# A transformer block on one core: butterfly weights laid out by partition, first steps reordered, second row group in the last score slots

## What is computed

```python
x = x + 0.5 * ffn(layernorm(x))
x = x + attention(layernorm(x))      # 16 heads of 16, causal, 4096 rows
x = x + 0.5 * ffn(layernorm(x))      # the same weights again
def ffn(x):
    h = butterfly(x @ W_exp + b_exp, up_weights)      # 1024 wide, 10 stages
    h = gelu(h + up_bias)
    return butterfly(h, down_weights) @ W_con + b_con + down_bias
def butterfly(y, weights):           # stage s pairs feature i with i + 2**s
    for stage in range(10):
        a, b = the two members of each pair; w = the pair's 2x2 matrix
        y = (w00 * a + w01 * b, w10 * a + w11 * b)
```

## Time and profile before

| what | value |
|---|---|
| median of 3 runs | 2031.27 us (2030.27 to 2039.89) |
| the profiled execution: its time | 2032.39 us |
| its span in the profile | 2030.7 us |
| PE busy | 1960.6 us, 97% |
| DVE busy | 1692.8 us, 83% |
| ACT busy | 1362.3 us, 67% |
| POOL busy | 342.3 us, 17% |

### The profile page before, as it was taken

How to read it: one execution, slowest core, us unless ns; L and a number is a source line. 1 busy time by engine, 2 the same in 40 slices (tenths; PEclk the granted TensorE clock), 3 DMA queues, 4 the chain that set the end, 5 groups by cost and what they waited for, 6 DMA issues and landing times.

```text
span 2030.7 us, 59085 instructions
## 1 busy us (share of the span) xinstructions
PE 1960.6 (97%) x24312; PEld 1206.0 (59%) x24312; DVE 1692.8 (83%) x3661; ACT 1362.3 (67%) x1640; POOL 342.3 (17%) x787
## 2 busy tenths in 40 slices
PE   2799999999999999999999999999999999999999
PEld 1677777655555555555555555555555555569998
DVE  7755566599999999999999999999999999736663
ACT  3422122288888888888888888888888888774444
POOL 6400000010111111011111101011110111124444
PEclk9899999999999999999999999999999999999999
DMA  7112111221111111111111111111112111101110
GB/s 192 42 67 82 50 50 50 85 67 40 42 51 42 47 46 43 42 40 52 41 46 44 45 44 40 52 41 45 41 45 47 40 51 33 51 28 61 53 53 22
DMA packets 93245, 104.26 MB, mean 51 GB/s; under 512 B 25552, under 2 KB 55856, under 8 KB 92720
## 3 DMA queue, kind: packets, MB, share of 16 engines
q1 hardware_dynamic: 92272, 100.23, 17.4%
q0 software_dynamic: 704, 0.25, 0.2%
HBM read 70.54 MB, written 29.36 MB: 49 GB/s over the span
## 4 chain that ended last, share of the span: by engine, by line
PE 91%; DVE 3%; SPq 2%; ACT 1%; DMA 1%; issue 1%; POOL 0%; POOLq 0%; ACTq 0%; DVEq 0%
PE PS L1167 32%; PE PS L1288 32%; PE PS L1144 7%; PE PS L1268 6%; PE PS L1114 6%; PE PS L1347 4%; PE PS L1219 2%; PE PS L1080 1%; PE PS L1138 1%; SPq L388 1%; DVE OA L829 1%; POOL QT L600 0%; ACT OA L631 0%; SPq L392 0%; DVE OA L934 0%
## 5 line engine op out<-in xcount | busy, mean ns | idle before, releaser
L722 ACT ACTIVATE PG<-PS 128x1024 f32<-128x1024 f32 (+1 forms) x1152 | 1117.1, 977 | 239.0 <-PE PS L1268 176.8
L958 DVE TENSOR_REDUCE MXP<-PS 128x1 f32<-128x512 f32 x1792 | 1099.2, 684 | 18.2 <-PE PS L1167 18.1
L1268 PE MATMUL PS<-QT,KT 50*128 50x512 f32 (+1 forms) x2304 | 811.1, 432 | 0.0
L1167 PE MATMUL PS<-KT,QT 48*128 48x512 f32 (+3 forms) x2304 | 797.1, 431 | 2.8 <-DVE MXP L958 2.3
L1288 PE MATMUL PS<-PG,VH 128*17 128x128 f32 x16896 | 726.1, 276 | 0.1
L1288 PEld LDWEIGHTS PS<-PG,VH 128*17 128x17 f32 x16896 | 400.2, 97 | 415.5 <-issue 367.2
L1167 PEld LDWEIGHTS PS<-KT,QT 48*128 48x128 f32 x2304 | 340.8, 184 | 251.2 <-issue 142.4
L1268 PEld LDWEIGHTS PS<-QT,KT 50*128 50x128 f32 x2304 | 339.5, 185 | 10.3 <-issue 10.1
L954 DVE CUSTOM_DVE_ANT_0 PS<-PS,MASK 128x128 f32<-128x128 f32 (+3 forms) x512 | 249.1, 505 | 73.4 <-PE PS L1167 67.7
L580 POOL TENSOR_SCALAR_AFFINE_SELECT PG<-PG 128x128 f32<-128x128 f32 x512 | 136.4, 292 | 999.3 <-ACT PG L722 998.5
L652 ACT ACTIVATE PG<-PS,GB 128x512 f32<-128x512 f32 x128 | 89.8, 706 | 161.9 <-PE PS L1114 161.9
(11 more groups left out here) (122 smaller groups left out, 1263.6 us busy)
## 6 DMA issues: line engine op xcount, KB each, us to landing
QT<-q_parts SPq DMA_DIRECT2D x256, 64.0 KB
KT<-k_parts SPq DMA_DIRECT2D x256, 64.0 KB
q_parts<-OA SPq DMA_DIRECT2D x16, 512.0 KB, 2.8
QT<-q_parts SPq DMA_DIRECT2D x256, 32.0 KB
k_parts<-OA SPq DMA_DIRECT2D x16, 512.0 KB, 4.9
KT<-k_parts SPq DMA_DIRECT2D x256, 32.0 KB
o_parts<-OS SPq DMA_DIRECT2D x128, 64.0 KB
OA<-o_parts SPq DMA_DIRECT2D x32, 256.0 KB
```

What stands on the lines that cost most here:

```text
L722: nc.scalar.activation(PB[n % 2][half][:, :, q0:TILE], PS[:, half * 1024:half * 1024 + 1024].rearrange("p (k q) -> p k q", k=2)[:, :, q0:T ...
L958: nc.vector.tensor_reduce(dst, bank(b), AX.X, ALU.max).then_inc(mx_red, 1)
L1167: mm(bank(4 + qs % 2 if b is None else b, w), q[0:SC, (BT * place(j) + qs) * P:(BT * place(j) + qs + 1) * P].bitcast(f32r), k[0:SC, c * TI ...
L1268: last = mm(PS[:, (2 * half + k) * 512 + q0:(2 * half + k + 1) * 512], CK[0:SM, kb * P:(kb + 1) * P].bitcast(f32r), CQ[0:SM, place(j) * TI ...
```

## The change

1. The host lays the inner weights out by partition (`by_partition`), so that a partition's half of every stage is one contiguous run. A stage is one DMA with a broadcast source. `inner_product` has one multiplication a stage, six in all; stage 0 is the loaded weights themselves. `beta`, `nbeta`, `identb` and the product's memsets go.
2. SP issues up stages 0, 2, 4, 6, ACT issues 1, 3, 5, ahead of its first work. POOL issues no weights; SP issues all seven down stages before w_con and then waits for w_con.
3. Scratch in OA and V moves, so that mixing may start while blocks are still being folded. ACT and DVE mix stage 0 of the up weights in pairs of blocks during the fold; DVE waits for the outer weights (`in_d`) before it finishes the first statistics, and ACT at its second block.
4. GB and OB on DVE move behind `low_weights` and behind the down mixing. ACT mixes the first down stage before the first GELU, with the GELU table loaded by a dummy activation before; the other two stages stand between the GELUs 2 to 5. Another dummy activation loads the GELU table before tile 1.
5. POOL also sets NK rows 32 to 63 (rows 96 to 127 of KT) to 1. In the last 23 slots the second matmul of each half reads NK and NQ in place of CK and CQ. For that the last head's maximum rows are loaded to NQ as well (four more DMAs each for the last two loads), and PE waits for them (`m_ld_n`).

```diff
 def w_offset(s):
-    return 32 * (2 ** s - 1)
+    return 2 * HB * (2 ** s - 1)
...
+            cur = F["w"]
+            eng.wait_ge(loaded[0], 16)
+            for s in range(1, INNER):
                 n = 2 ** s
+                w = F["w"][:, w_offset(s):w_offset(s + 1)].rearrange("p (b o c) -> p b o c", b=HB, o=2)
+                new = F["a"][s % 2][:, 0:HB * 2 * n].rearrange("p (b o c) -> p b o c", b=HB, o=2)
+                over_o = cur[:, 0:HB * n].rearrange("p (b c) -> p b c", b=HB).unsqueeze(2).to_broadcast([P, HB, 2, n])
+                eng.wait_ge(loaded[s], 16)
+                link(eng.tensor_tensor(new, w, over_o, ALU.mult))
+                cur = F["a"][s % 2]
...
         def inner_weights(eng, src, dst, s, sig):
             n = 2 ** s
+            rows = src[s].rearrange("a e -> (a e)").rearrange("(g x) -> g x", x=HB * 2 * n)
+            eng.dma_start(dst[:, w_offset(s):w_offset(s + 1)],
+                          rows.unsqueeze(1).to_broadcast([P // n, n, HB * 2 * n])).then_inc(sig, 16)
...
                 if t == 1:
+                    for s in range(INNER):
+                        inner_weights(sp, down_w, FD["w"], s, in_down[s])
                     sp.dma_start(WC[:, :, :], w_con.rearrange("(b p) d -> p b d", p=P)).then_inc(in_wc, 16)
-                    for s in range(DOWN_BY_POOL, INNER):
-                        inner_weights(sp, down_w, FD["w"], s, in_down[s])
-                    sp.wait_ge(in_down[INNER - 1], 16 * INNER_DMAS[INNER - 1])
+                    sp.wait_ge(in_wc, 16)
...
+                for to, sig in ((CQ, m_ld[g]), (NQ, m_ld_n[g])) if i >= 2 * (H - 1) else ((CQ, m_ld[g]),):
+                    rows = to[SC:SM, c0:c0 + S // 2].rearrange("a (b q t) -> a b q t", b=half, q=BT)
+                    for q in range(BT):
+                        sp.dma_start(rows[:, :, q, :], MT[g][q * Q32:(q + 1) * Q32, :]).then_inc(sig, 16)
...
             pool.wait_ge(md_ps, 4)
+            nc.gpsimd.memset(NK[NEXT // 2:NEXT, :], 1.0)
             nc.gpsimd.memset(CK[NEXT // 2:NEXT, :], 1.0).then_inc(att_init, 1)
...
+            for b in range(HB):
+                take_fold((b,))
+                if b == 1:
+                    act.wait_ge(in_d, 48)
+                if b % 2:
+                    act.wait_ge(fold_ev, b + 1)
+                    mix_a_side(0, (0,), (b - 1, b))
+                if b == 3:
+                    std(0, slice(0, 2 * BT))
+            mix_a_side(0, (1, 2))
...
+            nc.scalar.activation(SQRT_FIRST[:, :], ident[:, 0:1], ACT.Gelu)
+            act.wait_ge(in_wc, 16)
+            mix_a_side(1, (0,))
             act.wait_ge(gb_rdy, 1)
...
-                    for k in range(3):
-                        gelus(0, 0, (2 * k, 2 * k + 1))
-                        mix_a_side(1, (k,))
+                    gelus(0, 0, (0, 1))
+                    for b, k, mixed in ((2, 1, range(0, 2)), (3, 1, range(2, 4)), (4, 1, range(4, 8)),
+                                        (5, 2, range(0, 4))):
+                        mix_a_side(1, (k,), mixed)
+                        gelus(0, 0, (b,))
+                    mix_a_side(1, (2,), range(4, 8))
...
+            dve.wait_ge(in_d, 48)
+            finish_stats(0, slice(0, 2 * BT), 2 * BT, 2 * BT, lambda: mix_v_side(0, (0,), range(0, 4)))
             normalize(XN, 0, None)
+            mix_v_side(0, (0,), range(4, 8))
+            mix_v_side(0, (1, 2))
             take_transposed_parts(0, seq_f(0))
...
                     low_weights()
+                    dve.wait_ge(mix_v, 3 * HB)
+                    nc.vector.tensor_tensor(GB[:, :], T1[:, :, D], UB[:, :], ALU.add).then_inc(gb_rdy, 1)
                     dve.wait_ge(gb_rdy, 1)
                     dve.wait_ge(in_wc, 16)
                     mix_v_side(1, range(3))
+                    dve.wait_ge(in_bias, 32)
+                    link(nc.vector.tensor_tensor(OB[:, :], OB[:, :], OB2[:, :], ALU.add))
+                    nc.vector.tensor_scalar(OB[:, :], OB[:, :], 0.5, None, ALU.mult).then_inc(ob_rdy, 1)
...
+                last_slots = h * NCH + n >= H * NCH - AHEAD
...
                     kb = c * BT + 2 * half + k
+                    kt, qt = (NK, NQ) if last_slots and k else (CK, CQ)
+                    last = mm(PS[:, (2 * half + k) * 512 + q0:(2 * half + k + 1) * 512], kt[0:SM, kb * P:(kb + 1) * P].bitcast(f32r),
+                              qt[0:SM, place(j) * TILE + q0:(place(j) + 1) * TILE].bitcast(f32r), start=True, stop=True)
```

More of the change, by code:

```diff
@@ L299, in block_at, with inner_product @@
             return slice(t * BT + b, t * BT + b + 1)
-        def inner_product(eng, F, link, loaded, behind):
-            cur = F["a"][1]
-            for s in range(INNER):
+        def inner_product(eng, F, link, loaded):
+            cur = F["w"]
+            eng.wait_ge(loaded[0], 16)
+            for s in range(1, INNER):
                 n = 2 ** s
[L306 to L324, removed]
+                w = F["w"][:, w_offset(s):w_offset(s + 1)].rearrange("p (b o c) -> p b o c", b=HB, o=2)
[4 more added lines that the diff above has]
+                cur = F["a"][s % 2]
         A_FINAL = (INNER - 1) % 2
@@ L400, in _ @@
                 sp.sem_inc(parts_out[w], 16)
-            for s in range(INNER):
-                if s != UP_BY_POOL:
-                    inner_weights(sp, up_w, FU["w"], s, in_up[s])
+            for s in range(0, INNER, 2):
+                inner_weights(sp, up_w, FU["w"], s, in_up[s])
             sp.dma_start(WE[:, :, :], w_exp_t.rearrange("(b p) d -> p b d", p=P)).then_inc(in_we, 16)
@@ L523, in _ @@
                 sp.wait_ge(m_ld[g], 16 * BT * H)
+                sp.wait_ge(m_ld_n[g], 16 * BT)
         @block.gpsimd
@@ L542, in _ @@
                                     pattern=[[-1, TILE + 3 * P]], channel_multiplier=1).then_inc(const_rdy, 1)
[L543 to L547, removed]
+            inner_product(nc.gpsimd, FD, link, in_down)
             pool.sem_inc(a_down, 1)
@@ L611, in _ @@
             act.sem_inc(v_ev, FREE_V)
+            for s in range(1, INNER, 2):
+                inner_weights(nc.scalar, up_w, FU["w"], s, in_up[s])
             act.wait_ge(const_rdy, 1)
@@ L623, in std, with mix_a_side @@
                 nc.scalar.activation(LN[:, 3, cols], LN[:, 2, cols], ACT.Sqrt).then_inc(std_rdy, 1)
-            def mix_a_side(down, stages):
+            def mix_a_side(down, stages, blocks=range(HB)):
                 for k, b, ia, ib, wa, wb in mix_steps(down):
-                    if k not in stages:
+                    if k not in stages or b not in blocks:
                         continue
@@ L762, in _ @@
             nc.vector.memset(MXP[:, :, :], -3e38)
[L763 to L772, removed]
+            inner_product(nc.vector, FU, link, in_up)
             dve.sem_inc(a_up, 1)
@@ L785, in _, with finish_stats @@
                 first_stats(t)
-            def finish_stats(k, cols, w, done, before_std=(), here=False):
+            def finish_stats(k, cols, w, done, before_std=None, here=False):
                 def step(ins, n):
@@ L803, in finish_stats @@
                 nc.vector.scalar_tensor_tensor(L[2], L[2], 0.25, L[1], ALU.mult, ALU.add).then_inc(var_rdy, 1)
-                for item in before_std:
-                    maximum0(*item)
+                if before_std:
+                    before_std()
                 if here:
@@ L832, in normalize, with mix_v_side @@
                 last.then_inc(xn_rdy, 1)
-            def mix_v_side(down, stages):
+            def mix_v_side(down, stages, blocks=range(HB)):
                 for i, (k, b, ia, ib, wa, wb) in enumerate(mix_steps(down)):
-                    if k not in stages:
+                    if k not in stages or b not in blocks:
                         continue
+                    if k == 0 and not down:
+                        dve.wait_ge(fold_ev, (b | 1) + 1)
                     if k:
@@ L1264, in scores @@
                 q0 = 2 * P if j == c and half else 0
+                last_slots = h * NCH + n >= H * NCH - AHEAD
+                if half == 0 and h * NCH + n == H * NCH - AHEAD:
+                    pe.wait_ge(m_ld_n[0], 16 * BT)
+                if half == 0 and last_slots and c == j and j == ORDER[FIRST_ROWS]:
+                    pe.wait_ge(m_ld_n[1], 16 * BT)
                 pe.wait_ge(exp_done[half], h * NCH + n + 1)
@@ L1267, in scores @@
                     kb = c * BT + 2 * half + k
-                    last = mm(PS[:, (2 * half + k) * 512 + q0:(2 * half + k + 1) * 512], CK[0:SM, kb * P:(kb + 1) * P].bitcast(f32r),
-                              CQ[0:SM, place(j) * TILE + q0:(place(j) + 1) * TILE].bitcast(f32r), start=True, stop=True)
+                    kt, qt = (NK, NQ) if last_slots and k else (CK, CQ)
+                    last = mm(PS[:, (2 * half + k) * 512 + q0:(2 * half + k + 1) * 512], kt[0:SM, kb * P:(kb + 1) * P].bitcast(f32r),
```

(6 more changed lines are left out.)

57 lines of the change are left out of this document (11 added, 46 removed).

## The result

The changed kernel takes 2011.92 us (median of 5 runs) against 2031.27 before: ratio 0.9895, 95% interval 0.9876 to 0.9913. It is faster, by 19 us where 31 were forecast (2000; range 1992 to 2016). Repeated beside the experiments it took 2009.81 (ratio 0.9891, 0.9876 to 0.9905). The first profiled execution took 2014.8 us, with a span of 2013.0 against 2030.7 before; the repeat's profiled span was 2006.8.

What follows compares the result with a forecast made beforehand. PE bounds the bulk, which the change leaves alone; gains come at both ends. 17.5 + 9.3 - 2.1 + 6.5 = 31.2 us off 2032.39 gives 2001.2, median 2000; range 1993 to 2009, or 1992 to 2016 with the first two rivals.

Steps and rivals of the forecast that it cites:

- M = 31: Start: DVE's up mixing ends at 31 us against 48.5 before, gaining 17.5 us.
- x is late: Start: after the shorter fold, x becomes the late input, its second tile landing near 14.5 us.
- the bound 20.5 from a full queue: Start: upper bound for x's second tile landing, if DD's issue still takes 6.22 us with the queue full.
- the lower bound of the gain, 8.5: Start: smallest gain expected from an earlier end of the up mixing, 8.5 us of a range to 20.5.
- the first rival: Start: DU and DD's tiny runs keep x behind a full queue; mixing ends at 37, time 2006 us; 18%.
- x stays behind the full queue: Start: DD's issue keeps its 6.22 us, up mixing ends at 37, time 2006 us; 18%.
- The middle, 9.3: From mixed up weights to first output block: moving GB, OB and ACT's work gains 9.3 us (7 to 10).
- The stall of 2.1 at the third block: Tile 0's output blocks: POOL's added NK setting delays the residual, so PE waits; cost 2.1 us (0 to 3.5).
- The last slots, 6.5 with at most 9: Last 23 slots: score pairs on two row groups run side by side, slot 2.44 to 2.19 us; gain 6.5 (0 to 9).
- at most 8.3: Last 23 slots: most that shorter ACT waits could give back, 3.0 us at five waits plus 5.3 at 19 others.
- The slower rival: Last slots: TensorE's clock drops because PE is less busy, giving 2043 us or more; 2%.

Runs made afterwards that it cites:

- KT before the wait: Changed kernel with POOL's two settings of KT to 1 moved ahead of its wait for the last down fold: 2008.05 us, ratio 0.9875.
- the two combinations: Changed kernel, stages 5 and 6 split by source row, KT set first; outer weights behind x (2001.18 us) or in long runs (2001.05 us).
- one row group: Changed kernel with all score matmuls of the last 23 slots on CK and CQ again, extra loads kept: 2020.20 us, ratio 0.9938.

## Why the prediction was right or wrong

**Right in direction and in most terms, 12 us off in the sum.** By its own steps:

- *M = 31: wrong; 43.8.* It is the step "x is late": "near 14.5 for the second", with the bound 20.5 from a full queue. x was in at 28.8, beyond the bound and 14.3 us late; from there to M it took 15.0 us in place of my 16.5, so only the landing failed. My reason was that 1000 runs became 128 and half the bytes, so the transfers must be faster. What I did not look at is the shape of the source: with stage 6, of two source rows, under way, only two engines were at work (0.14 of 16), and W_exp, DU and x came late behind it. Splitting it by row brought M to 35.2 with nothing else changed. That shows the cause for 8.6 of the 12.8 us. The next 1.8 are the outer weights ahead of x (33.4 when behind). The last 2.4 are, in that kernel, x at 15.8 in place of 14.5, and 17.6 us from there to M in place of 16.5, with POOL's product on the mixing; they weren't taken apart further. The old kernel loaded stages 3 to 6 by one transfer per source row and had no such cost. A slip beside it: the lower bound of the gain, 8.5, doesn't follow from x at 20.5, which makes M 37 and the gain 11.5, as the first rival has it.
- The Trainium skill, "DMA: Bandwidth & Descriptors", in the section on why a DMA increments its semaphore by 16, says that a transfer runs on the largest number of engines up to 16 that divides the outermost dimension of both sides. For stage 6 that is two, for stage 5 four. The 0.14 of 16 engines at work, and the split's result, agree; stage 6 split alone agrees by its intermediate place. I had used that page for a bandwidth and not for this rule.
- *The rival "x stays behind the full queue"* named the right symptom (DU's issue took 11.91 us) with the wrong cause: DU's tiny runs. With stages 5 and 6 split they cost 5.5 us of SP's time and little of x's.
- *The middle, 9.3: right, 9.6, and 10.9 in the repeat* (output blocks 25.7 in place of 35.3 behind the mixing). The order on ACT, the price of 3.30 for a group of copies, and GB and OB moved all came as written.
- *The stall of 2.1 at the third block: right, 2.17 of PE's waiting and 2.3 us of delay.*
- *The last slots, 6.5 with at most 9: mis-sized; 9.5 and 9.6.* The mechanism was right. ACT's pace is 0.995 per exponential, not 1.09, so an ordinary slot falls from 2.44 to 1.99, and the "at most 8.3" was no bound. The new wait for the maxima cost nothing visible.
- *Clock: not in the sum.* The first profile loses 4.9 us between the first two maxima, at a lower clock; the repeat, the same code, loses 0.1.
- *The slower rival (clock falling in the last slots): no.* From 1740 us on the clock showed no such stretch. But its counterargument, that the tile loop keeps its clock, was wrong: the kernel before itself stood at 0.69 from 390 to 400 us.

With the repeat's profile the sum is 14.2 + 9.6 = 23.8 of a 23.9 us shorter span. In that profile M came 12.3 late (43.3 for 31), while the middle gave 1.6 more than forecast (the output blocks stand 24.4 behind the mixing) and the slots 3.1. So 4.7 us of the miss at the start were made good by terms that had been priced too low, which is luck.

## What to carry to other kernels

A transfer made of fewer, longer runs can be slower, as stage 6 was: look at the outermost dimension of both sides, and split a broadcast load by source row if it is small, above all when other loads stand behind it in the same queue. A start that waits for loads is bound by the last needed one, so price the whole queue ahead of it. When POOL has a long setting or sum to do, its place matters more than its length: put it where DVE doesn't normalise.

## What the runs showed of the hardware that I had not expected

- *DMA.* One transfer of 512 KB with an outer source dimension of 2 was in 17 us after its issue; as two transfers of 256 KB, beside the four of stage 5, 8 us until DVE went on with it.
- *POOL and DVE.* Two of POOL's settings of 32x4096 elements (3.5 us each), behind a product of 2.41, held a one-operand DVE instruction with two per-partition scalars (9.78 us for four in place of 1.4), and POOL's two-operand sum of 2.40 held it too (3.41). The same setting did not hold DVE's two-operand product (0.42 us beside it), nor its mixing (eight in 3.26 us beside it in the kernel with KT before the wait, 3.26 without). POOL's product did hold the mixing (20 in 11.12 us in place of 8.02). Of these three the setting, which reads nothing, held the normalisation alone.
- *Clock.* In two executions of the same kernel TensorE ran at its lower level (1.2 GHz) for different lengths at the start of attention, after a stretch in which PE had been busy for some 6 of 10 us at the end of the tile loop. First the changed kernel, then its repeat:

```profile
390.00:405.00 15.00, 14.90 (x125) 7.18 (x129) 10.18 (x17) 7.71 (x9) 1.70 (x8) 0.55 0.39 124
```

```profile
380.00:400.00 20.00, 19.75 (x184) 13.10 (x183) 13.78 (x24) 12.62 (x17) 2.53 (x12) 0.93 0.39 133
```

The first stood at 0.55 for 15 us and lost 4.9 us between the first two maxima; the second lost 0.1. Added up from the granted clock between 360 and 410 us, the lower level lasts some 17 us in the first profile; some 7 in the repeat, the kernel before, the split and most others; 10 and 14 us in the two combinations, in KT before the wait and in one row group, which lose some 2 us between the same maxima. In the split kernel the wait of 2.17 us before the third output block was followed by two blocks partly at the lower clock (0.67 from 70 to 74 us), 8.86 us in place of 7.17; behind the same wait in the changed kernel, its repeat and the one with outer weights behind x they took 7.17, so the wait alone doesn't decide it. Why the length differs from execution to execution stays open; it moves a time by some 5 us, as much as the smaller edits here.
